# One program of four layers: layer 0 interleaved over batches, the delta rule's output on VectorE alone, layer 3's experts on three engines

## The reference

```
x = x + L0_attn(layernorm(x)); x = x + L0_ffn(layernorm(x)); ... ; x = x + L3_attn(layernorm(x)); x = x + L3_ffn(layernorm(x))
```

## Time and profile before

| what | us |
|---|---|
| median of 3 runs (lowest, highest) | 4045.51 (4043.83, 4047.17) |
| the profiled execution, own time | 4041.39 |
| its span | 4039.7 |
| busy: TensorE, VectorE, ScalarE, GpSimd | 2893.5, 2158.6, 1212.7, 1108.7 |
| mean granted TensorE clock | 0.857 of full speed |

### The profile page before, as it was taken

How to read it: one execution, slowest core, us unless ns; L and a number is a source line. 1 busy time by engine, 2 the same in 40 slices (tenths; PEclk the granted TensorE clock), 3 DMA queues, 4 the chain that set the end, 5 groups by cost and what they waited for, 6 DMA issues and landing times. The chain is left out here.

```text
span 4039.7 us, 31623 instructions
## 1 busy us (share of the span) xinstructions
PE 2893.5 (72%) x9416; PEld 1546.9 (38%) x9416; DVE 2158.6 (53%) x3840; ACT 1212.7 (30%) x1826; POOL 1108.7 (27%) x644
## 2 busy tenths in 40 slices
PE   2004888799999889999678778638898985664334
PEld 1002334455555544444344433424444443343211
DVE  6777431222222356655444482147777775566676
ACT  1001333211111146666343203314444442221000
POOL 0002554200000000000123203119899884453000
PEclk8556888899999989999788889858999997887569
DMA  1001112000000075555000021120000000000000
GB/s 46 0 0 27 42 48 50 19 0 0 0 0 0 0 149 142 140 145 142 10 0 1 8 58 48 49 53 0 0 0 0 0 0 21 0 0 1 0 6 21
DMA packets 103181, 124.26 MB, mean 31 GB/s; under 512 B 21611, under 2 KB 55532, under 8 KB 102796
## 3 DMA queue, kind: packets, MB, share of 16 engines
q1 hardware_dynamic: 101004, 118.56, 11.5%
q0 software_dynamic: 2048, 4.20, 0.3%
HBM read 108.55 MB, written 14.16 MB: 30 GB/s over the span
## 5 line engine op out<-in xcount | busy, mean ns | idle before, releaser
L2044 POOL TENSOR_TENSOR dots_pr<-dots_g 128x1536 f32<-128x1536 f32 (+1 forms) x129 | 394.1, 3095 | 117.6 <-DVE dots_g L2149 78.0
L2070 PE MATMUL dots_fold<-dots_pr,all_ident 128*128 128x512 f32 x688 | 322.8, 616 | 2.7 <-ACT dots_pr L2110 2.7
L795 DVE SCALAR_TENSOR_TENSOR attn_sim<-attn_sc,attn_mask 128x512 f32<-128x512 f32 (+3 forms) x256 | 125.8, 492 | 316.9 <-PE attn_sc L725 313.8
L725 PE MATMUL attn_sc<-attn_q,attn_xb 128*128 128x512 f32 (+3 forms) x768 | 295.0, 486 | 0.0
L736 PE MATMUL attn_op<-attn_sim,attn_v 128*128 128x512 f32 (+3 forms) x768 | 295.0, 486 | 0.0
L1069 DVE TENSOR_TENSOR grp_h<-grp_sq,grp_cb 128x512 f32<-128x512 f32 x256 | 176.5, 692 | 195.1 <-ACT grp_sq L961 171.0
L908 PE MATMUL grp_po<-grp_h,grp_down 128*128 128x512 f32 x512 | 266.1, 602 | 7.7 <-DVE grp_h L1069 7.7
L900 PE MATMUL grp_ph<-all_xt,grp_up 128*128 128x512 f32 x512 | 263.6, 597 | 5.9 <-DMA grp_sdown<-L_ffn_shared_down_w_dram 5.9
L2146 DVE TENSOR_TENSOR dots_m<-dots_pu,dots_sg 128x512 f32<-128x512 f32 x256 | 164.7, 685 | 162.4 <-ACT dots_sg L2101 155.5
L468 POOL TENSOR_TENSOR mix_h<-mix_r,mix_cb 128x512 f32<-128x512 f32 x128 | 187.5, 1479 | 154.9 <-ACT mix_r L418 124.4
L955 ACT ACTIVATE grp_r<-grp_ph 128x512 f32<-128x512 f32 x272 | 162.4, 597 | 191.9 <-PE grp_ph L900 190.2
(11 more groups left out here) (602 smaller groups left out, 5158.3 us busy)
## 6 DMA issues: line engine op xcount, KB each, us to landing
grp_cb<-grp_combine SPq DMA_DIRECT2D x512, 128.0 KB, 3.2
mix_cb<-top_weights SPq DMA_DIRECT2D x64, 256.0 KB, 3.4
cap_xs<-cap_zero SPq DMA_DIRECT2D x7, 320.0 KB, 4.3
experts_xe<-cap_xs SPq DMA_DIRECT2D x7, 320.0 KB, 3.4
cap_w<-in_L_ffn_W_dram SPq DMA_DIRECT2D x1, 2048.0 KB
cap_ys<-experts_yo SPq DMA_DIRECT2D x8, 256.0 KB, 2.3
delta_h<-all_xn SPq DMA_DIRECT2D x1, 2048.0 KB
all_xn<-delta_h SPq DMA_DIRECT2D x1, 2048.0 KB, 8.6
```

What stands on the lines that cost most here:

```text
L725: nc.tensor.matmul(sc[k % SC][:, 0:w], xb[:, m * P:(m + 1) * P], q[:, par, n0:n0 + w], start=True, stop=True).then_inc(s_mm, 1)
L2044: nc.gpsimd.tensor_tensor(slot[U % SLOTS][:, r0 + i0:r0 + i0 + n], g[:, I % 2, a0:a0 + n, hs], key, ALU.mult).then_inc(pp_ready, 1)
L2070: ins = nc.tensor.matmul(fold[U % NU][:].rearrange("p (n h f) -> p n h f", h=HQ, f=FW), ident[:], slot[U % SLOTS][:, :, :, f * FW:(f + 1) ...
```

## The change

Three parts, put into one kernel.

1. *Layer 0.* X is loaded by batch inside the stage (`load_x`), batch 0 first, 1 after the small weights, 2 and 3 last. Both whole-array norms before the stage go. The two norms in a row become one: `statistics_in(b)` and `normalise_in(b)` on VectorE by batch, with the root of (1 + 1e-5) * var + 1e-10 on ScalarE (`deviation_in`), and weight and bias applied when ScalarE takes the transposes to XT. Transposes of all kinds share the one PSUM buffer `tr` in an order written out by hand (`tr_use`, semaphore `tr_free`). `experts(b)` on TensorE, ScalarE and GpSimd now calls `beside(b + 1, m)` at each step m: the work of the next batches stands at fixed steps between the products. Logits and turned weights use `po` instead of `ph`. wT has two buffers. The wait after each correction goes, with one wait in `gated` instead. VectorE's order is interleaved anew.
2. *Delta rule's output.* GpSimd has no part. VectorE makes all products (`part`, three buffers) and sums. Loops are unrolled, so the copies of XT and alpha go. TensorE's order is: turn sum n, value products of the next block, project sum n - 1.
3. *Layer 3's experts.* Even tiles stay with VectorE; for odd tiles ScalarE multiplies (eight activations with scale into `part`) and GpSimd folds the 1024 columns (512, 256, 128) and adds to X. PSUM has four pairs instead of two. After each group of four tiles SyncE stores it; the last block goes.

```diff
-    OUT_COPY_AT, OUT_TURN_AT, OUT_SPREAD_AT = 2, 6, 8
+    OUT_COPY_AT, OUT_TURN_AT = 2, 5
+    LAST_TURN, NORM_IN, PROJECT, MIXED, GATES, STD, TURN_IN, LOGITS, EXP, REACH, SPREAD_W = 1, 2, 4, 9, 10, 13, 15, 18, 21, 20, 27
...
+                def beside(p, m):
+                    if p > 1 and m == LAST_TURN:
+                        turn_out(GPB * (p - 1) - 1)
+                    if p + 1 < BATCH:
+                        if NORM_IN <= m < NORM_IN + GPB:
+                            turn("norm", p + 1, m - NORM_IN, ixn_ready)
+                        if PROJECT <= m < PROJECT + CT:
+                            inputs(p + 1, m - PROJECT)
+                        if GATES <= m < GATES + CT:
+                            gates(p + 1, m - GATES)
+                    if p < BATCH:
+                        if m == MIXED:
+                            output(p)
+                        if TURN_IN <= m < TURN_IN + GPB:
+                            turn("in", p, m - TURN_IN, xn_ready)
+                        if m == LOGITS:
+                            logits(p)
+                        if m == SPREAD_W:
+                            turn_weights(p)
+                    if m == NH + OUT_TURN_AT:
+                        turn_out(GPB * (p - 1))
...
+                for b in range(BATCH):
+                    for m in range(GPB * NH):
+                        weigh(b * GPB * NH + m)
+                        if m == REACH and b + 2 < BATCH:
+                            largest(b + 2)
+                        if m == LAST_TURN + LAG and b:
+                            add_out(b * GPB - 1)
+                        if m == NH + OUT_TURN_AT + LAG:
+                            add_out(b * GPB)
...
                     stt(gk, q[:, :, 1], w, gk, ALU.mult, ALU.add).then_inc(fix, 1)
-                    dve.wait_ge(fix, done + 4)
-                    dve.sem_inc(fix, 1)
...
+                for b in range(1, BATCH):
+                    scan(b, 0)
+                    scan(b, 1)
+                    add_mixed(b - 1)
+                    scan(b, 2)
+                    normalise(b - 1)
+                    scan(b, 3)
+                    reaches(b)
+                    if b + 1 < BATCH:
+                        statistics_in(b + 1)
+                    route(b - 1)
+                    gains(b)
+                    take_masks(b)
+                    if b + 1 < BATCH:
+                        normalise_in(b + 1)
+                    corrections(b)
+                    gated(b)
...
+                            ins = tt(acc[:, n % 2], v[:, j % 2, 0], bcast(alpha[:, t, 0, j], D_), ALU.mult)
+                            ins.then_inc(acc_first if t else acc_ready, 1)
+                            if n >= 1:
+                                dve.wait_ge(acc_ready, n)
+                            for r in range(1, t + 1):
+                                tt(part[:, r - 1], v[:, j % 2, r], bcast(alpha[:, t, r, j], D_), ALU.mult).then_inc(part_ready, 1)
...
+                                ins = tt(acc[:, n % 2], acc[:, n % 2], part[:, r - 1], ALU.add)
+                                ins.then_inc(added if r < t else acc_ready, 1)
+                            finish(j * S + t - 2)
...
+                for g in range(NG):
+                    sp.wait_ge(vec_added, (g + 1) * TPG // 2)
+                    sp.wait_ge(pool_added, (g + 1) * TPG // 2)
+                    sp.dma_start(out_dram[:, g * TPG:(g + 1) * TPG], X[:, g * TPG:(g + 1) * TPG]).then_inc(x_out, 16)
...
+                    for e in range(E):
+                        ins = nc.scalar.activation(part[:, k % 2, e * C:(e + 1) * C], po[i % SETS][e // EPB][:, (e % EPB) * C:(e % EPB + 1) * C],
+                                                   ACT.Identity, scale=coef[:, i, e:e + 1])
...
+                    w_ = E * C // 2
+                    while w_ >= C:
+                        c.link(nc.gpsimd.tensor_tensor(part[:, k % 2, 0:w_], part[:, k % 2, 0:w_], part[:, k % 2, w_:2 * w_], ALU.add))
+                        w_ //= 2
+                    nc.gpsimd.tensor_tensor(X[:, i], X[:, i], part[:, k % 2, 0:C], ALU.add).then_inc(pool_added, 1)
```

More of the change, by code:

```diff
@@ L362, in _ @@
                 pe.wait_ge(w_copied, 2)
[L363 to L377 removed]
+                for b in range(2):
+                    for g in range(GPB):
+                        turn("norm", b, g, ixn_ready)
+                    for k in range(CT):
+                        inputs(b, k)
+                    if b == 0:
+                        for k in range(CT):
+                            gates(0, k)
@@ L379, in _, with take_inputs @@
+                output(0)
+                for k in range(CT):
+                    gates(1, k)
+                for g in range(GPB):
+                    turn("in", 0, g, xn_ready)
+                logits(0)
+                turn_weights(0)
+                pe.wait_ge(w1_in, 32)
+                pe.wait_ge(w2_in, 32)
+                for b in range(BATCH):
+                    experts(b)
+                turn_out(NG - 1)
             @block.scalar
             def _(act):
-                def take_inputs(b):
+                def take_inputs(b, k):
@@ L606, in _ @@
                 dve.wait_ge(gates_in, 32)
-                for b in range(BATCH + 1):
-                    if b < BATCH:
-                        scans(b)
-                    if b:
-                        add_mixed(b - 1)
-                    if b < BATCH:
-                        for k in range(NSEG):
-                            c.link(ts(G[:, k], S[:, k], gain[:, k % CT:k % CT + 1], None, ALU.mult))
-                    if b:
-                        normalise(b - 1)
-                    if b < BATCH:
-                        dve.wait_ge(most_ready, b + 1)
-                        c.link(stt(flags[:], most[0:1].rearrange("p (s d) -> p s d", d=DS), BOUND * 0.999, bit[:], ALU.is_gt, ALU.mult))
-                        c.link(redu(mask_f[:], flags[:], AX.X, ALU.add))
-                        c.link(nc.vector.tensor_copy(masks[:], mask_f[:]))
-                    if b:
-                        route(b - 1)
-                    if b < BATCH:
-                        corrections(b)
-                        gated(b)
+                for k in range(NSEG):
+                    scan(0, k)
+                reaches(0)
+                statistics_in(1)
+                gains(0)
+                normalise_in(1)
+                take_masks(0)
+                corrections(0)
+                gated(0)
+                for b in range(1, BATCH):
[15 more added lines that the diff above has]
+                    gated(b)
+                add_mixed(BATCH - 1)
+                normalise(BATCH - 1)
+                route(BATCH - 1)
 def relu_attention(nc, X, XN, XT, ident, Wq, Wk, Wv):
@@ L2355, in turn, with values @@
-                    def turn(j, t):
-                        pe.wait_ge(acc_ready, j * S + (t + 1))
+                    def values(j, t):
+                        if j >= JT:
+                            return
+                        for half in range(2):
+                            n = (j * S + t) * 2 + half
+                            if n >= 2:
+                                pe.wait_ge(v_ready, n - 1)
+                            nc.tensor.matmul(pv[half][:], XTj[:, t, j], wv[:, half * GROUP:(half + 1) * GROUP], start=True, stop=True).then_inc(v_mm, 1)
@@ L2373, in _, with project @@
-                    pipelined(pe, prepare, rest)
+                    def project(n):
+                        if n < 0:
+                            return
+                        pe.wait_ge(lT_ready, n + 1)
+                        if n >= 2:
+                            pe.wait_ge(x_done, n - 1)
+                        for a in range(HD // P):
+                            ins = nc.tensor.matmul(po[n % 2][:, 0:C], lT[:, n % 2, a], woT[:, a], start=(a == 0), stop=(a == HD // P - 1))
+                        ins.then_inc(out_mm, 1)
@@ L2391, in rest @@
+                    for t in range(S):
+                        take(0, t)
+                    for j in range(JT):
+                        for t in range(S):
+                            n = j * S + t
+                            act.wait_ge(t_mm, n + 1)
+                            if n >= 2:
+                                act.wait_ge(out_mm, n - 1)
                             for half in range(2):
@@ L2393, in rest @@
                             ins.then_inc(lT_ready, 1)
-                    pipelined(act, prepare, rest)
+                            take(j + 1, t)
                 @block.vector
@@ L2648, in _ @@
-                dve.wait_ge(x_added, NT + 2)
+                c = Chain(dve, ch)
+                for k in range(NT // 2):
+                    i = 2 * k
+                    dve.wait_ge(out_mm, i + 1)
+                    for e in range(E):
+                        o = po[i % SETS][e // EPB][:, (e % EPB) * C:(e % EPB + 1) * C]
```

(5 more changed lines are left out.)

533 lines of the change are left out of this document (277 added, 256 removed).

## The result

The changed kernel takes 3812.92 us (median of 4 runs, 3805.09 to 3814.84), the kernel before 4045.95 in the same comparison: 0.9421 of the time, 95% interval 0.9405 to 0.9437. The forecast was 3835. The profiled execution is the fastest of the four, 3805.09 us with a span of 3803.3, so the two traces are 236.4 us apart.

The account below looks back on a forecast made before the run. Layer 0 was bound by VectorE's corrections, then TensorE's products; delta output by a GpSimd-VectorE ring; layer 3's experts by VectorE. Gains 106 + 40 + 62 = 208 off 4041.4 gave 3833, adjusted to 3835; range 3785 to 3900.

Parts of the forecast that it names:

- rival without lateness: Rival, chance 0.17: weights in time, GpSimd's way back free, folds at 2.9; gains 122, 55 and 72, 3793 us.
- Start: Layer 0: scans begin at about 20.0 us instead of 61.9, masks at 43.6 instead of 83.5; 40 us gained.
- Corrections: Layer 0, batch 0: without the wait, the branch walk hides under a 1.28 us instruction; 28 us gained, bounds 0-29.
- the cap: Upper bound on the corrections' gain: 12 long gaps give 15.4 us, 16 shorter ones 14.0, 29 at most.
- y(1) late by 4: Layer 0, experts of batch 0: y(1) at step 9 late by 4 us, with 12.4 us of skipped correction branches.
- Logits and ranks beside GpSimd: Layer 0: ranks beside GpSimd's multiplies take 0.5 us each, 17 us instead of 8; batch 1's weights late by 6.
- GpSimd's way back: Layer 0: return from a reduction to multiplies, twice, 0 to 5.8 us each, taken as 3, together 6.
- Delta output: Delta rule's output on VectorE without GpSimd: period 25.2 us, eight of them 202; gain 40, bounds near 5 to 60.
- Layer 3's experts: GpSimd last at 4.2 us a tile, 67 us; TensorE 55, VectorE 50; gain 62 us, bounds 52 to 73.
- Small operations held for whole multiplies: Rival, chance 0.17: some 54 small linked VectorE operations a batch cost 0.5 us more each; +45, 3880 us.
- TensorE's clock: Rival, chance 0.02: interrupted product streams are granted clock 0.50 instead of 1.00; 4138 us, slower than before.
- The walk isn't hidden: Rival, chance 0.12: at layer 0's corrections the sequencer does not run ahead through branches; +28, 3863 us.

Follow-up runs that it names:

- Experiment 3: Changed kernel with each correction's wait for its own last instruction put back; 3854.6 us, ratio 0.9536.
- experiment 4: Changed kernel with layer 0's maxima over partitions taken from GpSimd and done by TensorE and VectorE; 3809.0 us, ratio 0.9413.
- experiment 6: Changed kernel with one more GpSimd addition of 128 columns per odd tile in layer 3's experts, result unused; 3815.2 us, ratio 0.9432.
- experiment 8: Changed kernel with maxima off GpSimd, final addition three sums back, weights turned at step 29, layer 3's expert weights loaded earlier; 3764.0 us, ratio 0.9304.

## Why the prediction was right, and where it was not

The time is 22 us below the forecast of 3835 and 20 above the rival without lateness (3793), so the number alone does not pick the forecast's case. The three gains were forecast at 106, 40 and 62 and measured 110.3, 49.6 and 71.8; that rival had 122, 55 and 72. Layer 0 came near the forecast, the delta output in between, and layer 3's experts as the rival had them. Part of the nearness is luck: in layer 0 errors of both signs cancelled.

The parts of layer 0 are not equally well shown. The correction's wait was tried by itself. The earlier start (some 38 us, masks at 45.7 instead of 83.5) and the work beside the experts are read from the timelines, and so are the four PSUM pairs and the static addresses in layer 3's experts; none of these was run alone.

- **Start.** Right by 2 us. The scans started 2.6 later than forecast, as the projection and not VectorE was last.
- **Corrections.** The mechanism was right, the term too small: 32.5 us less between the first correction and the gating (248.6 before, 216.1 after), forecast 28 and at most 29. The step that was mis-sized is the cap: it took a gap's worth as what the gap showed. The 12 long gaps gave 17.0 us and not 15.4, as each lost up to 0.27 more than the 1.28. The 16 short ones sum to 14.8 in the trace of before, not to the 14.0 of the forecast, and gave 15.9: hidden, the next instruction also starts 0.07 before the last one ends, and a pair of corrections stood 8.02 us apart before and 7.21 after, 0.81 for a gap of 0.72. Experiment 3 puts 32.1 of the 32.5 on the wait by itself (248.2 against 216.1).
- **y(1) late by 4.** Wrong in the changed kernel: no wait. The forecast took the walk of 12.4 us from the batches before; it was 11.5, with `normalise_in` in it. That is 0.9 of the 4; the rest is not placed. Experiment 3, where the walk was 16.4, had the wait (4.58). So the mechanism is there, on an edge of 0.3 us that the length of the walk decides.
- **Logits and ranks beside GpSimd.** The 28 ranks took 13.3 us in the third phase, 0.48 each, forecast 0.5. The weights were late by 5.3, forecast 6, but in part from elsewhere: VectorE stood 7.2 us for the exp, which stands at step 21 in ScalarE's list; the forecast had 1.5 for it in the first batch and nothing here.
- **GpSimd's way back.** Forecast between 0 and 5.8, taken 3; measured 7.08 and 7.22, outside the bounds. The absence is 13.6 us instead of 9.8, TensorE stands 9.7 and 9.9 for it, and the second phase is 89.5 instead of 82.5 plus 3. Some of it is paid by the ranks, which run free meanwhile (experiment 4: taking two such waits out gives 8.8 us and not 19.6). The first phase (91.4 instead of 91.5 plus 3) and the third (74.5 instead of 77) were shorter than the forecast, and the corrections gave more, so the sum of layer 0 hid this.
- **Delta output.** The waits were right, 3.49 and 0.42 for 3.3 and 0.8. VectorE's own term was too large: a product is recorded with 1.22 us but the next starts 1.13 after it (the earlier trace rows had only single ones), so ten products a block are 1.1 us less, and the final additions 0.2 each instead of 0.33. 23.6 a block instead of 25.2 is some 12.7 over eight, and the longer waits of three blocks take some 3 back. The measured 49.6 is the best of five traces; the others have 41.6 to 48.0, nearer to the 40.
- **Layer 3's experts.** Wrong in the bound: GpSimd was forecast last with 4.2 us a tile and took 3.13 (2.60 for three folds with their links, 0.08 for a link, 0.45 for the last addition). The link is 0.08, where the forecast took 0.33 from the earlier trace rows, and the folds are shorter too. The rival without lateness had the folds at 2.9 and the gain at 72: it was nearer here. TensorE's 55 and VectorE's 0.39 were right, so TensorE came last; experiment 6 shows GpSimd with 0.3 us a pair to spare.
- **Small operations held for whole multiplies** (rival, 0.17). Half right: small operations are held for most of a multiply, 1.15 to 1.23 instead of 0.2 us, but only 7 of the 28 in the third phase; and what is lost is bounded, since a waiting TensorE lets GpSimd run dry. The Trainium skill, "SBUF — State Buffer", section "Who interferes with whom", calls the shared port pair an exclusive lock; the held ranks of experiment 8 (1.22 and 1.20 us beside multiplies of 1.26) agree with it.
- **TensorE's clock** (rival, 0.02). Not in the experts, where a product stays at 0.43. In the output stage the mean is near 0.9, and three of eight blocks take a few us more.
- **The walk isn't hidden** (rival, 0.12): excluded by the rows at 62.10 and by experiment 3.

## What to carry to other kernels

Hold a stream's cost per instruction as the distance of two starts in a run of such instructions, not as a recorded duration or a gap: the corrections and the delta output's products were both off by this. A wait for another engine's result belongs as late in the waiting engine's list as the buffers allow; one index moved from two to three was worth some 30 us. And before a bound engine is relieved by postponing a wait, look at what the wait gives to others: while TensorE stood, GpSimd ran dry and the ranks took 0.2 us each, where the held ones took 1.2.

## What the runs showed of the hardware

- GpSimd needs time on both sides of a partition reduction between ordinary multiplies: 6.01 and 6.04 us before it, 7.08 and 7.22 after it in the changed kernel. The time between the two multiplies, 13.6 and 13.8 us, is the firm number; where the reduction stands in it is a rough one. The Trainium skill, "GPSIMD Engine Reference", section "2.1 Instruction dispatch", has approximately 6 us for the first call of a freshly loaded kernel (there a routine of GpSimd's own); the way in agrees with that number, but is paid here both times, though the reduction had run twice before, and of a way back the section says nothing.
- VectorE's sequencer walks branches under a running instruction: a walk that showed as 0.7 to 1.5 us of idle time after a wait is hidden under an instruction of 1.28 us, and the next instruction starts 0.07 us before that one ends.
- The walk over 64 skipped positions, in two of three batches with `normalise_in` running in it, took between 11.3 and 16.4 us over the batches of nine kernels, none of which corrects anything in it, and went with the kernel. What sets it stayed open.
- The stage of the delta output, a stretch in which TensorE pauses some us in every block, scatters by 8 us between five profiles of the same code, all of it in VectorE's waits for TensorE, with the granted clock in single blocks between 0.86 and 0.93.
